# A bias of the feed-forward moved from four matmuls into the column bias of an activation

## The reference, cut to what matters

```python
h  = layernorm(x + agg, g1[l], beta1[l])                  # 512 x 256 per graph
ff = gelu(h @ W1[l] + b1[l]) @ W2[l] + b2[l]              # W1: 256 x 1024, W2: 1024 x 256
x  = layernorm(h + ff, g2[l], beta2[l])
```

## Time and profile before

| | us |
|---|---|
| median of 3 runs (2314.73 to 2318.89) | 2317.78 |
| profiled execution | 2312.36 |
| its span, first to last instruction | 2310.6 |
| TensorE busy / weight loads busy | 1937.2 / 1651.7 |
| VectorE busy | 1697.3 |
| ScalarE busy | 1166.5 |
| GpSimd busy | 915.7 |
| mean granted TensorE clock | 0.959 of 2.4 GHz |

### The profile page before, as it was taken

One profiled execution on the slowest core, in us unless ns is written; L12 is line 12 of the kernel. 1 busy time (PEld: TensorE's weight loads), 2 busy tenths in 40 slices (PEclk: granted clock), 3 DMA queues, 4 the chain that ended last, 5 costly groups with the idle time before them and its releaser, 6 DMA issues.

```text
span 2310.6 us, 34337 instructions
## 1 busy us (share of the span) xinstructions
PE 1937.2 (84%) x11201; PEld 1651.7 (71%) x11201; DVE 1697.3 (73%) x5031; ACT 1166.5 (50%) x1844; POOL 915.7 (40%) x661
## 2 busy tenths in 40 slices
PE   3888888997789978899778987889878898879994
PEld 2777676886678867787667776678767786668873
DVE  6666788667786777867777777776787767876655
ACT  2554555454555545555445554555545555555542
POOL 2345433443334443344333443334333444334442
PEclk9899989999999999999999999999989999999997
DMA  4001100001000010001000010000100001000000
GB/s 153 19 19 46 42 6 10 19 19 46 7 14 10 19 46 11 19 1 38 28 11 19 1 55 11 10 19 1 56 11 10 19 19 42 5 10 28 1 1 19
DMA packets 40909, 53.15 MB, mean 23 GB/s; under 512 B 2920, under 2 KB 31244, under 8 KB 40716
## 3 DMA queue, kind: packets, MB, share of 16 engines
q1 hardware_dynamic: 40716, 50.76, 6.7%
HBM read 42.36 MB, written 8.39 MB: 22 GB/s over the span
## 4 chain that ended last, share of the span: by engine, by line
PE 35%; issue 27%; POOL 16%; DVE 15%; ACT 5%; DMA 1%; POOLq 0%; SPq 0%; ACTq 0%; DVEq 0%
PE ps_d L470 11%; PE ps_a L405 9%; POOL gelu_lo L1207 5%; PE ps_u L444 5%; POOL x_nat L1183 3%; PE ps_a L500 2%; POOL probs L1213 2%; DVE junk L937 2%; ACT normed L652 2%; PE ps_t L414 2%; DVE probs L1009 2%; POOL rstd L1174 2%; ACT g_full L671 2%; PE ps_a L486 1%; PE ps_u L428 1%
## 5 line engine op out<-in xcount | busy, mean ns | idle before, releaser
L671 ACT ACTIVATE g_full<-ps_u,vec_col 128x512 f32<-128x512 f32 x384 | 258.6, 686 | 494.5 <-PE ps_u L444 269.2
L470 PE MATMUL ps_d<-w_hi,gelu_hi 128*128 128x256 f32 x1536 | 460.4, 300 | 37.2 <-POOL gelu_lo L1207 27.6
L470 PE MATMUL ps_d<-w_hi,gelu_lo 128*128 128x256 f32 x1536 | 439.7, 286 | 0.0
L470 PE MATMUL ps_d<-w_lo,gelu_hi 128*128 128x256 f32 x1536 | 438.9, 286 | 0.0
L1174 POOL TENSOR_TENSOR rstd<-var_eps,minus_half 128x4 f32<-128x4 f32 x128 | 135.4, 1058 | 695.3 <-DVE var_eps L795 695.3
L405 PE MATMUL ps_a<-x_nat,probs 128*128 128x257 f32 x1536 | 364.0, 390 | 36.4 <-DVE normed L880 33.5
L1207 POOL TENSOR_TENSOR gelu_lo<-g_full,gelu_hi 128x512 fp32r<-128x512 f32 x240 | 310.4, 1302 | 175.9 <-ACT gelu_hi L679 161.6
L405 PEld LDWEIGHTS ps_a<-x_nat,probs 128*128 128x128 f32 x1536 | 286.0, 192 | 107.9 <-DVE normed L880 42.4
L470 PEld LDWEIGHTS ps_d<-w_hi,gelu_hi 128*128 128x128 f32 x1536 | 299.1, 195 | 55.2 <-POOL gelu_lo L1207 38.3
L470 PEld LDWEIGHTS ps_d<-w_lo,gelu_hi 128*128 128x128 f32 x1536 | 297.4, 194 | 6.0
L470 PEld LDWEIGHTS ps_d<-w_hi,gelu_lo 128*128 128x128 f32 x1536 | 296.9, 193 | 0.0
(11 more groups left out here) (135 smaller groups left out, 3827.4 us busy)
## 6 DMA issues: line engine op xcount, KB each, us to landing
adj_in<-adj_dram SPq DMA_DIRECT2D x64, 256.0 KB, 2.9
x_nat<-x_dram SPq DMA_DIRECT2D x16, 512.0 KB, 4.0
x_res<-x_dram SPq DMA_DIRECT2D x16, 512.0 KB, 3.9
out_dram<-x_res SPq DMA_DIRECT2D x64, 128.0 KB, 1.7
x_res<-L_gnn_W_dram SPq DMA_DIRECT2D x5, 1024.0 KB, 5.2
probs<-L_gnn_W_dram SPq DMA_DIRECT2D x1, 1024.0 KB, 11.3
attn_row<-L_gnn_attn_w_dram SPq DMA_DIRECT2D x1, 768.0 KB
g_row<-L_gnn_g_dram SPq DMA_DIRECT2D x1, 384.0 KB
```

What stands on the lines that cost most here:

```text
L470: last = pe.matmul(ps_d[c // 2][:, cols:cols + D], h[:, r, tok], w[:, layer, f, :], start=False, stop=(f == FC - 1 and i == 2), skip_group ...
L671: full = act.activation(g_full[:, f % 2, :], ps_u[f % 2][:, :], ACT.Gelu, bias=b1_col[:, layer, f:f + 1])
```

## The change

b2 is loaded as six more rows of `vec_rows` (42 in all) and becomes columns like beta1. A new tile `both_col` holds beta1 + b2. h_full is made with the bias both_col, so the residual that goes into ps_d holds h + b2. h_hi keeps the bias beta1. The low part subtracts both: (h_full - b2) - h_hi, one operation with a scalar per partition. The four b2 matmuls of a step are gone, and with them ones_r, b2_parts, their three VectorE operations, and two memsets and two selects on GpSimd. VectorE makes both_col once behind its setup; ScalarE waits for it before its first `h_split`.

```diff
+        b2_col = vec_col[:, LAYERS * (FC + 2 * KC):VECS].rearrange("p (l c) -> p l c", l=LAYERS)
+        both_col = sb("both_col", [P, LAYERS, KC], F32)
...
-                (b2_all, b2.rearrange("(o l) d -> o l d", o=1).broadcast_to([P, LAYERS, D])),
+                (vec_rows[LAYERS * (FC + 2 * KC):VECS, :], b2.rearrange("l (c p) -> (l c) p", p=P)),
...
-                pe.matmul(dst[:, cols:cols + D], ones_r[:, :], b2_parts[:, layer, :], start=False, stop=False,
-                          skip_group_check=True)
...
-                    act.activation(h_full[:, k, :], ps_t[k][:, :], ACT.Identity, bias=beta1_col[:, layer, k:k + 1],
+                    act.activation(h_full[:, k, :], ps_t[k][:, :], ACT.Identity, bias=both_col[:, layer, k:k + 1],
                                    scale=g1_col[:, layer, k:k + 1]).then_inc(h_act.sem, 1)
...
+            act.wait_ge(both_ready.sem, both_ready.at(0))
             h_split(0, 0)
...
-                    dve.tensor_tensor(h_lo[:, k, :], h_full[:, k, :],
-                                      h_hi[:, k, :].bitcast(F32), ALU.subtract).then_inc(h_ready.sem, 1)
+                    dve.scalar_tensor_tensor(out=h_lo[:, k, :], in0=h_full[:, k, :], scalar=b2_col[:, layer, k:k + 1],
+                                             in1=h_hi[:, k, :].bitcast(F32), op0=ALU.subtract,
+                                             op1=ALU.subtract).then_inc(h_ready.sem, 1)
...
-            step(dve.tensor_copy(ones_r[:, :], ones_f))
-            step(dve.tensor_copy(b2_round, b2_all))
-            step(dve.scalar_tensor_tensor(out=b2_parts[:, :, :], in0=b2_round.bitcast(F32),
-                                          scalar=minus_row[:, 0:1], in1=b2_all, op0=ALU.mult, op1=ALU.add))
...
+            dve.wait_ge(vec_ready.sem, vec_ready.at(0))
+            dve.tensor_tensor(both_col[:, :, :], beta1_col, b2_col, ALU.add).then_inc(both_ready.sem, 1)
             attention_sum(0, 0, prepare=1)
...
-            pool.memset(ones_f, 1.0)
-            pool.memset(minus_row[:, :], -1.0)
...
-            pool.affine_select(out=ones_f, in_=ones_f, compare_op=ALU.is_ge, fill=0.0,
-                               base=1, pattern=[[0, P]], channel_multiplier=-1)
-            pool.affine_select(out=minus_row[:, :], in_=minus_row[:, :], compare_op=ALU.not_equal, fill=0.0,
-                               base=0, pattern=[[0, 1]], channel_multiplier=1)
```

More of the change, by code:

```diff
@@ L70, in gnn_program @@
         w_last = sb("w_last", [P, KC, D + 2], F32)
-        VECS = LAYERS * (FC + 2 * KC)
+        VECS = LAYERS * (FC + 3 * KC)
         vec_col = sb("vec_col", [P, VECS], F32)
@@ L75, in gnn_program @@
         g1_col = vec_col[:, LAYERS * FC:LAYERS * (FC + KC)].rearrange("p (l c) -> p l c", l=LAYERS)
-        beta1_col = vec_col[:, LAYERS * (FC + KC):VECS].rearrange("p (l c) -> p l c", l=LAYERS)
+        beta1_col = vec_col[:, LAYERS * (FC + KC):LAYERS * (FC + 2 * KC)].rearrange("p (l c) -> p l c", l=LAYERS)
+        b2_col = vec_col[:, LAYERS * (FC + 2 * KC):VECS].rearrange("p (l c) -> p l c", l=LAYERS)
+        both_col = sb("both_col", [P, LAYERS, KC], F32)
         attn_row = sb("attn_row", [P, LAYERS, 2, D], F32)
@@ L81, in gnn_program @@
         bias_col = sb("bias_col", [P, 2, LAYERS], F32)
-        b2_parts = sb("b2_parts", [P, LAYERS, D], F32R)
-        minus_row = sb("minus_row", [P, 1], F32)
-        ones_r = sb("ones_r", [P, P], F32R)
         ident = sb("ident", [P, P], F32)
@@ L141, in gnn_program @@
         a_row = normed[:, 0:2, :]
-        b2_all = wh[:, 0:LAYERS, 0:D]
-        ones_f = wh[:, LAYERS, 0:P]
         all_ones = h_last[:, 0, 0:P]
-        b2_round = h_last[:, :, :].rearrange("p k n -> p (k n)")[:, 0:LAYERS * D].bitcast(F32R).rearrange(
-            "p (l d) -> p l d", l=LAYERS)
         def bank(name):
@@ L163, in gnn_program @@
         vec_ready = sem("vec_ready")
+        both_ready = sem("both_ready")
         setup_v = sem("setup_v")
@@ L246, in gnn_program @@
             weight_loads.append((W2[l].rearrange("(k p) f -> p k f", p=P), w2_hi[:, l], w2_lo[:, l], FC, D))
-        SETUP = 3 + 6 * (LAYERS - 1) + 2 * KC
+        SETUP = 6 * (LAYERS - 1) + 2 * KC
         SMALL = 10
@@ L283, in _ @@
                 (vec_rows[LAYERS * FC:LAYERS * (FC + KC), :], g1.rearrange("l (c p) -> (l c) p", p=P)),
-                (vec_rows[LAYERS * (FC + KC):VECS, :], beta1.rearrange("l (c p) -> (l c) p", p=P)),
+                (vec_rows[LAYERS * (FC + KC):LAYERS * (FC + 2 * KC), :], beta1.rearrange("l (c p) -> (l c) p", p=P)),
                 (attn_row[:, :, :, :], attn_w.rearrange("(o l) (t d) -> o l t d", o=1, t=2).broadcast_to([P, LAYERS, 2, D])),
@@ L898, in attention_norm, with h_rest @@
                 dve.wait_ge(ln1_apply.sem, ln1_apply.at(n))
-            def h_rest(n):
+            def h_rest(n, layer):
                 for k in range(KC):
                     dve.wait_ge(h_act.sem, h_act.at(n, k + 1))
-                    dve.tensor_tensor(h_lo[:, k, :], h_full[:, k, :],
-                                      h_hi[:, k, :].bitcast(F32), ALU.subtract).then_inc(h_ready.sem, 1)
+                    dve.scalar_tensor_tensor(out=h_lo[:, k, :], in0=h_full[:, k, :], scalar=b2_col[:, layer, k:k + 1],
+                                             in1=h_hi[:, k, :].bitcast(F32), op0=ALU.subtract,
+                                             op1=ALU.subtract).then_inc(h_ready.sem, 1)
                 dve.wait_ge(h_ready.sem, h_ready.at(n))
@@ L1090, in _ @@
             assert count[0] == SETUP
+            dve.wait_ge(vec_ready.sem, vec_ready.at(0))
+            dve.tensor_tensor(both_col[:, :, :], beta1_col, b2_col, ALU.add).then_inc(both_ready.sem, 1)
             attention_sum(0, 0, prepare=1)
             attention_norm(0)
-            h_rest(0)
+            h_rest(0, 0)
             def pair_body(pair, first, last):
@@ L1151, in pair_body @@
                     if attend:
-                        h_rest(n + 1)
+                        h_rest(n + 1, layer_a)
             each_pair(dve, pair_body)
```

## The result

The changed kernel takes 2326.38 us (median of 6 runs, 2325.29 to 2333.66), the kernel before 2315.89 in the same series (6 runs, 2312.88 to 2318.89). The ratio is 1.005, 95% interval 1.0035 to 1.0064: slower, by some 10 us. The forecast was 2320, with "no change" the likeliest case. The profiled execution of the changed kernel took 2326.46, its span is 2324.7.

What follows compares the result with a forecast made beforehand. The prediction took a ring of waits across TensorE, ScalarE, VectorE and GpSimd as the bound, with the b2 matmuls beside it. Matmuls 0, scalar +3.7, start -1.4 gave +2.3 on 2317.8, so 2320 us, range 2310 to 2330.

Steps and rivals of the forecast that it cites:

- The range: Whole kernel: measured time expected between 2310 and 2330 us.
- the sum: Whole kernel: 0 for matmuls, +3.7 for the scalar, -1.4 for the start, together +2.3 us.
- Matmuls, gain 0: TensorE's down(0): dropping four b2 matmuls frees 0.48 us a step, which only widens later waits; gain on the path 0.
- The price of one: One b2 matmul in down(0) costs TensorE's queue 0.12 us, with 0.21 as upper bound.
- Rival A: TensorE, busy 84%, bounds after all, so all 192 matmuls pay: 2294 us; chance 0.10.
- The scalar, 0.06 us: VectorE's h_lo: the scalar form takes 0.75 instead of 0.692 us, 0.06 more each; 3.7 us in all.
- The route over GpSimd: The second h_lo's 0.06 us delay reaches the path through GpSimd's rstd and gelu_lo, despite VectorE's 0.30 us slack.
- The upper bound: Scalar term: h_lo at most 0.33 us longer each, less the 0.30 slack, about 12 us in all.
- C: VectorE's h_lo: scalar free or absorbed by 0.30 us slack, only the start counts: 2316 us; chance 0.12.
- The start, -1.4: Loads and setup before the first step: b2 loaded once as 3 KB, fewer VectorE operations; -1.4 us, load bounds 0 and 1.6.
- wrong in the mechanism if a step's length moves by over 0.2 us: The prediction's own failure sign: any step's length changing by over 0.2 us in either direction.
- Rival B: TensorE's wider waits call up another half-clock stretch per pair, 9 us on top: 2329 us; chance 0.17 slower, 0.01 within.

Runs made afterwards that it cites:

- e3: Changed kernel plus 24 transposes that nobody reads in TensorE's first wait, putting the loop back where it was before; 2310.37 us, ratio 0.9968.
- e10: Changed kernel plus only 8 transposes in TensorE's first wait of the start; 2310.4 us, ratio 0.9957.
- e1: Kernel before with only the four b2 matmuls left out (b2 missing from the result); 2329.94 us, ratio 1.0058.
- e7: Kernel before without the four b2 matmuls (b2 missing), plus 24 transposes that keep the loop's place; 2312.66 us, ratio 0.9986.
- e5: Changed kernel with 24 transposes at the start and h_lo by plain subtraction again (b2 also counted in the low part); 2309.62 us, ratio 0.9975.
- e12: Kernel before with the scalar form (zero column) for the first h_lo of a step alone; 2316.19 us, ratio 1.0002.
- e2: Kernel before with only h_lo computed in the scalar-column form, the column being zero; 2325.31 us, ratio 1.0032.
- e6: Changed kernel plus 88 transposes in TensorE's first wait of the start; 2313.2 us, ratio 0.9988.
- e8: Kernel before with the zero-column scalar h_lo and 128 transposes at the start, loop moved by 256 instructions; 2325.52 us, ratio 1.0042.
- e11: Kernel before with the zero-column scalar h_lo and 64 transposes at the start, loop moved by 128 instructions; 2324.94 us, ratio 1.0029.

## Why the prediction was right or wrong

The range held 2326.4, and that is luck: the sum had +2.3 us, and the 16 us that made the time came from a place that no term and no rival named. Without them the changed kernel takes 2310.4 (e3, e10), at the other end of the range and faster than before. Step by step:

- **Matmuls, gain 0.** Right: e1 and e7 leave the regular step at 36.32 to 36.36, the waits took 0.25 and 0.21 us as worked out. The price of one was right too: from chunk 0 to chunk 1 of down(0) it is 0.72 us with the b2 matmul (1313.60 to 1314.32) and 0.61 without (1287.72 to 1288.33), so 0.11 each. Against "gain 0" stand the 3 us of e7, which came through the clock. Rival A (2294) is refuted by e7's 2312.7. The Trainium skill, Perfetto Trace Analysis, "Identifying the Most-Contended Engine", says to improve the engine with the highest occupancy first, but also that the busy share of matmuls is no good measure, and takes the achieved rate of work and the share of weight loads for it. The trace bears out the warning: by matmuls TensorE leads (84%), by weight loads it has 71%, less than VectorE's 73%, and removing 192 of its matmuls gave 3 us, those by the clock.
- **The scalar, 0.06 us.** The size is right: 750 against 692 ns. The place is right as far as the runs tell: from e5 to e3 both h_lo together cost 0.06 a regular step, and from e12 to e2 the second alone costs as much, so nothing is left for the first. The route over GpSimd fits (its rstd starts 3.15 us into the step instead of 3.11). But a regular step grew by 0.10: the other 0.04 was in no term, and e5 has it without any scalar. The term was 3.7 us; 0.10 in 47 steps is 4.7, at most 1 more. The upper bound does not come out of its own figures: 0.33 for each of 28 h_lo and 0.03 for each of 34 is 10 us, not 12. C is refuted in the steps; e12's median shows how little of it a measurement of the whole tells.
- **The start, -1.4.** Right in sign, small in size: the first step begins at 58.5 to 60.8 in the six profiles with the new start (median 59.0), and at 60.4 to 64.0 in the eight with the old (61.4), so 2.4 us rather than 1.4, with a scatter as large. In the changed kernel's own profile the first dot products moved from 19.25 to 17.42 and the first scores from 31.00 to 29.18, 1.8 each, and the DMA engines are still 89% busy from 10 to 15. The row in order of time, then the stretch:

```profile
17.42 0.48 DVE L821 CUSTOM_DVE_ANT_0 junk<-x_nat,attn_row,bias_col 128x256 bf16<-128x256 f32 x1 [4.81 <-DMA bias_col<-L_gnn_attn_b_dram]
```

```profile
10.00:15.00 5.00, 0.00 (x0) 0.00 (x0) 1.37 (x9) 2.50 (x5) 1.02 (x1) 1.00 0.89 310
```

- **What was missing.** "Sum +2.3" left out the turn of the loop, +16 us by e3 and e10. The turn was in view: the earlier trace rows has VectorE's "issue" of 3.07 us there, which I read as fixed (it is 3.30 in the changed kernel). This is the step that failed: I did not look at TensorE's "issue" at the same turn, 1.65 us, nor ask what the 48 instructions that leave the program ahead of the loop would do to it. My own alarm, "wrong in the mechanism if a step's length moves by over 0.2 us", went off: +2.98 in sixth steps.
- **Rival B (2329, slower).** Its number was nearest, its mechanism is not what happened. The half-clock stretch that lengthens a second step comes with the stall and goes with it: e3 has the same wide waits (0.64 and 1.3) and second steps of 47.46 with a mean clock of 0.959, and of the 25 short turns in kernels with these waits (e3, e5, e6, e7, e10) one alone, the longest (2.20 us, in e6), is followed by a long second step (48.36). Half clock right behind the turn is no sign of the stall by itself: it stands behind all 20 stalled turns, but also behind 19 of the 50 short ones, one of them in the kernel before. In e2 a mechanism like it is real, but it came from the longer subtraction with all matmuls in place, with waits that had not widened (0.40 and 1.08). The Trainium skill, TensorE: Matmul & The Clock Gate, "HAM oscillation", ties the lower clock to idle time of the array. The turn fits it (4.7 us idle, then 0.50). e2's fifth step does not decide by it: 1.58 us idle in a pair that falls and in one that doesn't.

The parts do not add. Against the kernel before, at a good place: matmuls out -3 us (e7), scalar alone +7 to +10 (e2, e8, e11), matmuls out, new start and scalar together -3 to -10 (e6, e3, e10), the bad place +16 to +19 on top. The traces account for only part of the -3 to -10: e3's span is 1.9 us shorter than that of the kernel before, whose profiled execution (2312.4) was one of its fastest. The change itself, read without its accident of place, is a gain of 0.1 to 0.4%: e6 0.9988, e3 0.9968, e10 0.9957 (0.9942 to 0.9973). e3 or e10 is the version to keep. Eight transposes are enough.

## What to carry to other kernels

When an edit changes how many instructions an engine has ahead of or in a hardware loop, its effect is confounded with the loop's place: read the "issue" idle time of the first instruction behind the loop's turn in both traces before believing a difference of a few tenths of a per cent, and move the loop with a few idle instructions in a wait to separate the two. Here 16 instructions in a wait (e10) were worth 16 us, more than any other part of the change. And measure step by step: equal steps next to one that grew by 3 us point at the cause at once, while busy times (1937.2 and 1936.9) say nothing.

## What the runs showed of the hardware that was not expected

- A turn of the loop costs TensorE 1.6 to 2.2 us, or 4.4 to 5.6 at a bad place; 16 instructions decide between them (-48 bad, -32 good), and the bad place repeats after 256. At the bad place two instruction blocks of 16 KB are fetched one after the other ahead of the first matmul (20 of 20 turns), else one (50 of 50).
- A subtraction with a scalar column takes 750 ns for 512 float32 elements against 692 without.
- The lower clock can lock to the program: in e2, e8 and e11 it fell in the same alternate pairs, whatever the start (60.39 to 63.45 us); 0.06 us less a step (e12) went with the end of the pattern.
